# AdaLN block with attention on one core: first weights in chunks, TensorE multiplies zeros until they come, new order of work up to the first scores

## The reference

```python
mod = (silu(c) @ wmod).reshape(4, 6, 1, 512)          # sa, ca, ga, sb, cb, gb
h = layernorm(x) * (1 + ca) + sa
q = rope(h @ Wq.T);  c_kv = h @ Wdk.T                 # Wdk: 512 x 512
k = rope parts from h @ Wkr.T, the rest from c_kv @ Wupk.T
v = c_kv @ Wupv.T
x = x + ga * (softmax(causal(q @ k.T) / sqrt(128)) @ v) @ Wo.T
h = layernorm(x) * (1 + cb) + sb
x = x + gb * (h * sum(top8 of softmax(router)) + chosen weights @ expert_bias)
```

## Time and profile before

| | us |
|---|---|
| median of three runs | 1457.12 |
| the runs | 1459.28, 1457.12, 1456.52 |
| span of the profiled execution | 1457.5 |
| TensorE busy | 1430.5 (98%) |
| VectorE, ScalarE, GpSimd busy | 1153.7, 1006.8, 1023.1 |
| chain that ended last, TensorE's share | 85% |

### The profile page before, as it was taken

One profiled execution on the slowest core, in us unless ns is written; L12 is line 12 of the kernel. 1 busy time (PEld: TensorE's weight loads), 2 busy tenths in 40 slices (PEclk: granted clock), 3 DMA queues, 4 the chain that ended last, 5 costly groups with the idle time before them and its releaser, 6 DMA issues.

```text
span 1457.5 us, 24651 instructions
## 1 busy us (share of the span) xinstructions
PE 1430.5 (98%) x7150; PEld 1208.2 (83%) x7150; DVE 1153.7 (79%) x3544; ACT 1006.8 (69%) x2389; POOL 1023.1 (70%) x805
## 2 busy tenths in 40 slices
PE   7989999999999999999999999999999999999998
PEld 7877888888888888888888888888888888888886
DVE  5697777777777777787777777777779998998876
ACT  5667666776776676767676677677677676776674
POOL 3767766876776677667676767677588888887662
PEclk9999999999999999999999999999999999999999
DMA  9478765875677667676677667758788899889872
GB/s 305 157 210 250 225 193 182 239 235 152 204 227 218 187 212 228 190 206 211 184 216 233 220 180 208 202 178 257 228 239 259 269 295 262 284 256 270 270 229 67
DMA packets 215157, 322.03 MB, mean 221 GB/s; under 512 B 42512, under 2 KB 132464, under 8 KB 215024
## 3 DMA queue, kind: packets, MB, share of 16 engines
q1 hardware_dynamic: 214736, 320.39, 73.7%
q10 hardware_dynamic: 288, 0.07, 0.0%
HBM read 179.43 MB, written 140.95 MB: 220 GB/s over the span
## 4 chain that ended last, share of the span: by engine, by line
PE 85%; POOL 4%; DVE 4%; DMA 2%; issue 2%; ACT 2%; SPq 0%; DVEq 0%; ACTq 0%
PE bank_s L634 22%; PE bank_o L794 21%; PE bank_pv L744 14%; PE bank_s L700 13%; PE bank_s L666 5%; PE bank_s L651 5%; POOL PT_lo L1836 2%; PE bank_s L696 1%; PE bank_s L607 1%; PE bank_s L850 1%; DVE y L1540 1%; DMA PT_raw<-blocks 1%; POOL qT_lo L1829 1%; DMA wc_scratch<-wc_out 1%; DVE blocks L1488 0%
## 5 line engine op out<-in xcount | busy, mean ns | idle before, releaser
L1836 POOL TENSOR_TENSOR PT_lo<-PT_raw,PT_hi 128x640 fp32r<-128x640 f32 x246 | 382.2, 1576 | 30.4 <-ACT PT_hi L1126 30.4
L1112 ACT ACTIVATE probs<-probs,row_inv 128x512 f32<-128x512 f32 (+3 forms) x512 | 257.8, 553 | 192.1 <-DVE row_inv L1471 192.1
L1824 POOL TENSOR_TENSOR rot_c<-rot_c,rot_s 128x512 f32<-128x512 f32 x128 | 167.7, 1310 | 257.7 <-DVE rot_s L1428 257.7
L1105 ACT ACTIVATE probs<-probs,row_min 128x384 f32<-128x384 f32 (+3 forms) x512 | 281.6, 552 | 49.2 <-DVE row_min L1464 49.2
L1488 DVE STREAM_TRANSPOSE blocks<-probs 128x384 f32<-128x384 f32 x508 | 213.7, 446 | 21.2 <-ACT probs L1112 13.0
L700 PE MATMUL bank_s<-kT_both,qT_hi 128*128 128x512 f32 (+2 forms) x768 | 215.2, 341 | 3.0 <-issue 1.3
L1464 DVE CUSTOM_DVE_ANT_0 probs<-bank_s,mask 128x512 f32<-128x512 f32 (+2 forms) x384 | 205.5, 552 | 0.8 <-issue 0.3
L1829 POOL TENSOR_TENSOR qT_lo<-rot_c,qT_hi 128x512 fp32r<-128x512 f32 x128 | 167.0, 1304 | 51.0 <-ACT qT_hi L1087 50.2
L634 PE MATMUL bank_s<-hT_lo,wq_hi 128*128 128x512 f32 x484 | 194.8, 403 | 2.2 <-DVE row_min L1464 1.4
L794 PE MATMUL bank_o<-wo_lo,OT_hi 128*128 128x512 f32 x496 | 195.1, 393 | 0.5 <-DVE rot_s L1428 0.5
L794 PE MATMUL bank_o<-wo_hi,OT_hi 128*128 128x512 f32 x496 | 193.4, 390 | 0.0
(11 more groups left out here) (315 smaller groups left out, 3255.0 us busy)
## 6 DMA issues: line engine op xcount, KB each, us to landing
blocks<-blocks SPq DMA_DIRECT2D x127, 640.0 KB, 3.5
PT_raw<-blocks SPq DMA_DIRECT2D x500, 160.0 KB, 3.9
stage<-in_wq SPq DMA_DIRECT2D x32, 256.0 KB, 5.1
vblocks<-kv_raw SPq DMA_DIRECT2D x32, 256.0 KB, 5.4
kv_raw<-vblocks SPq DMA_DIRECT2D x128, 64.0 KB, 2.3
stage<-in_wo SPq DMA_DIRECT2D x32, 256.0 KB, 5.1
split_wq<-wq_hi SPq DMA_DIRECT2D x32, 256.0 KB, 5.4
split_wq<-wq_lo SPq DMA_DIRECT2D x32, 256.0 KB, 5.7
```

The lines of the kernel that those rows point to most:

```text
L1105: ins = act.activation(row(t, qt), row(t, qt), ACT.Exp, bias=row_min[m][:, qt:qt + 1], scale=-1.0, accum_out=row_sum[m][:, qt:qt + 1])
L1112: ins = act.activation(row(t, qt), row(t, qt), ACT.Copy, scale=row_inv[t % 2][:, qt:qt + 1])
L1824: pool.tensor_tensor(rot_c[:], rot_c[:], rot_s[:], ALU.add).then_inc(pool_a, 1)
L1836: pool.tensor_tensor(lo[:, at], raw_of(t)[:, at], hi[:, at].bitcast(F32), ALU.subtract).then_inc(pool_t, 1)
```

## The change

It touches only the stretch before the loop.

1. The first quarter of Wup is loaded in four chunks (SyncE), Wdk in four chunks of 128 columns instead of 128 rows, the first of them on ScalarE's queue. The splits follow chunk by chunk: up 0, down 0, up 1, 2, 3, down 1, 2, 3. `combine(0)` starts with the first two.
2. VectorE clears `kv_rot` first, and TensorE multiplies its zeros 9 times (fp32, 128 x 128) before `combine(0)`.
3. The exponential for silu and what follows it stand behind the splits. `ident` is loaded by SyncE, later.
4. All lists are rewritten up to `scores(2)`; `transpose_h(4)` to (7), `statistics(1)` to (3), `normalise_x(1)` to (3) and the loads of x stand later, combines and the first keys and queries earlier. Beyond `combine(15)` the lists are as they were.

```diff
+WARM_UPS = 9
+UP_FIRST, DOWN = [1, 3, 4, 5], [2, 6, 7, 8]
...
 def h_bank(n):
-    return bank["s1" if n % 2 == 0 else "o2"] if n < 2 * CH else bank["o2" if n % 2 == 0 else "o3"]
+    if n < 2 * CH:
+        return bank["o2" if n % 2 else "s1" if n < CH else "o3"]
+    return bank["o2" if n % 2 == 0 else "o3"]
...
+def warm_up():
+    pe.wait_ge(dve_pro, 1)
+    for _ in range(WARM_UPS):
+        pe.matmul(bank["pv"][:, 0:P], kv_rot[:, 0:P], kv_rot[:, P:2 * P], start=True, stop=True)
 def combine(i):
-    if c == 0:
-        pe.wait_ge(split_lo, n + 1 + (CH if n > 0 else 0))
+    if n == 0 and c > 0:
+        pe.wait_ge(split_lo, DOWN[c])
+    elif c == 0 and n > 0:
+        pe.wait_ge(split_lo, 2 * CH + n)
     for m in range(CH):
         if i == 0:
-            pe.wait_ge(split_lo, m + 2)
+            pe.wait_ge(split_lo, max(UP_FIRST[m], DOWN[0]))
...
+def split_down(c):
+    cols = slice(c * P, (c + 1) * P)
+    act.wait_ge(d_wdk[c], 16)
+    act.activation(wdk[0][:, :, cols], wdk_in[:, :, cols], ACT.Copy).then_inc(split_w, 1)
```

More of the change, by code:

```diff
@@ L586, in transpose_h @@
                     pe.wait_ge(d_ident, 16)
+                if n == CH:
+                    pe.wait_ge(dve_kr, 1)
                 if n == 2 * CH:
@@ L919, in tensor_program @@
             combine(2)
+            combine(3)
+            combine(4)
             modulation(0)
-            combine(3)
+            combine(5)
+            combine(6)
             modulation(1)
@@ L1253, in scalar_program @@
             combine(1)
-            normalise_x(0)
             combine(2)
             combine(3)
+            combine(4)
+            normalise_x(0)
+            combine(5)
+            combine(6)
+            split_first(0)
+            split_up(2)
             split_h(0)
[L1258 to L1261, removed]
             split_h(1)
[L1263 to L1266, removed]
             combine(7)
             split_first(1)
+            split_h(2)
+            split_h(3)
             combine(8)
+            combine(9)
             split_first(2)
[L1271 to L1274, removed]
             split_up(3)
-            split_h(6)
             k_split(0)
+            normalise_x(1)
+            combine(10)
+            q_split(0)
             split_first(3)
             split_first(4)
-            combine(10)
-            q_split(0)
-            split_h(7)
+            q_split(1)
+            split_h(4)
+            split_h(5)
             combine(11)
-            q_split(1)
-            split_first(5)
             exponentials(0, 0)
             exponentials(0, 1)
+            split_first(5)
             combine(12)
+            split_h(6)
+            split_h(7)
             normalise(0, 0)
             normalise(0, 1)
-            normalise_x(3)
+            normalise_x(2)
             q_split(2)
@@ L1299, in scalar_program @@
             q_split(3)
+            normalise_x(3)
             split_h(8)
@@ L1696, in vector_program @@
             modulate_h(0)
+            modulate_h(1)
+            split_up(2)
+            modulate_h(2)
+            modulate_h(3)
             statistics(1)
[L1698 to L1704, removed]
             dve.wait_ge(dve_pro, ROT_CLEAR)
@@ L1707, in vector_program @@
             k_rope(0)
-            modulate_h(6)
             dve.wait_ge(d_const, 64)
             q_rope(0)
-            modulate_h(7)
-            statistics(3)
+            split_up(3)
             q_rope(1)
-            split_up(3)
+            modulate_h(4)
+            modulate_h(5)
             mask_and_max(0, 0)
             mask_and_max(0, 1)
+            statistics(2)
             q_rope(2)
@@ L1719, in vector_program @@
             invert_sums(0, 1)
+            modulate_h(6)
+            modulate_h(7)
             transpose_blocks(0)
@@ L1722, in vector_program @@
             mask_and_max(1, 1)
+            statistics(3)
             q_rope(3)
```

150 lines of the change are left out of this document (83 added, 67 removed).

## The result

| | before | changed |
|---|---|---|
| median, us | 1457.97 (6 runs, 1456.52 to 1459.51) | 1462.28 (6 runs, 1460.67 to 1464.89) |
| span of the profiled execution | 1457.5 | 1459.6 |
| TensorE busy | 1430.5 | 1433.2 |

The ratio is 1.0028, interval 1.0017 to 1.0038: slower by 4.3 us in the medians, where 2.1 us less were forecast.

The account below looks back on a forecast made before the run. TensorE was taken as the bound: its moment past 117.22 plus a fixed 1340 us. A 5.5 us lead, less 0.9 and 0.9, plus 0.8, less 2.4, left 2.1: 1457.1 - 2.1 = 1455.0 us, range 1451.2 to 1458.4.

Parts of the forecast that it names:

- The 2.6 us for the zeros: Before combine(0): nine zero products raise TensorE's clock early, saving 2.6 us of slow matmuls, within bounds of 0 to 2.8.
- q_rope(1) runs from 46.3, mask_and_max(0) 49.9 to 51.8: New lists before scores(2): start of q_rope(1) and VectorE's next step, in us, after normalise_x(1) delays q_split(0) on ScalarE.
- plus 0.8 of short waits around 54 to 59 that are no longer there: Term of the sum: TensorE's short waits at 54 to 59 us vanish, adding 0.8 us to the lead.
- Plus a fixed rest of 1340 us: After TensorE's wait at 117.22: the remaining time was taken as a constant 1340 us, whatever the start gains.
- a pause of 1 us: TensorE's pause between zeros and combine(0): no row showed such a pause in the loop bringing slow matmuls back.
- Only the loads decide: Rival, chance 0.12: the wait at 117.22 hangs on load_transposed(0), only 0.7 us ahead, giving 1456.4 us.
- Slower: Rival, chance 0.09: narrow packets and a later list place make x 0 late, delaying combine(15); 1460.6 us.

Follow-up runs that it names:

- e4: The changed kernel with GpSimd's low part of the fifth weight piece moved ahead of q_rope(1); 1460.81 us, ratio 1.0008.
- e5: The changed kernel run again unaltered, in a later comparison against the kernel before; 1463.18 us, ratio 1.0035.
- e11: The kernel before with only GpSimd's fifth weight piece moved behind q_rope(1), as in the changed list; 1464.28 us, ratio 1.0041.
- e10: The kernel before with 64 waits on a finished load added at SyncE's step 20, nothing changed ahead of 117; 1458.21 us, ratio 1.0000.
- f3: The changed kernel with constant products filling TensorE's pauses at k_proj(0), q_proj(2) and near 92, 96 and 117 us; 1460.56 us, ratio 1.0011.
- e1: The kernel before with only the early clearing of kv_rot and the nine zero products added; 1459.98 us, ratio 1.0006.
- f1: The kernel before with constant products filling TensorE's three pauses near 93, 97 and 117 us; 1458.83 us, ratio 0.9999.
- e7: The changed kernel with SyncE's load_transposed(0) moved ahead of the store of combine(15); 1461.73 us, ratio 1.0025.
- f2: The changed kernel's start (chunks, slices, zeros) with the old lists, TensorE's pauses near 91, 95 and 116 us filled; 1459.65 us, ratio 1.0006.
- f4: The changed kernel with GpSimd's fifth piece ahead of q_rope(1), pauses at k_proj(0) and near 91, 95, 116 us filled; 1460.95 us, ratio 1.0015.
- e6: The changed kernel with ScalarE's normalise_x(3) moved behind combine(15); 1462.89 us, ratio 1.0030.

## Why the prediction was wrong

**The start: right, in part by luck.** combine(0) 5.91 (6.9), zeros ended before it, one table load, combine(2) ended at 12.8 (13.1), transpose_h(0) 23.51 (23.9), x in time, combine(8) and k_proj(0) waited 0.63 and 1.67 and ran at 28.43 and 34.54 (29.1, 34.2). The 2.6 us for the zeros was too much: 1.1. combine(0) started 1.0 us earlier than forecast, but combine(1) had to wait until 8.50 for the low part of its slice; these two errors largely cancel at 12.8. And about 1 us of the gain was the baseline's: the profile from which it was counted reached combine(3) at 19.84, others of that start at 18.75 to 19.15.

**The lists: the first failed step.** It is "q_rope(1) runs from 46.3, mask_and_max(0) 49.9 to 51.8", and the sum's "plus 0.8 of short waits around 54 to 59 that are no longer there". The step followed VectorE and ScalarE and left GpSimd's next entry out: the fifth piece stands behind q_rope(1) in the new list, and q_proj(2) waits for it. The short wait of 0.38 there did not vanish, it became 2.57. Alone, that order is worth 0.8 to 1 us at 117 (e4 against the changed kernel and e5, whose starts agree within 0.2 us), and in the kernel before it cost 5.6 us (e11). The other part is q_rope(1) itself, 48.09, of which GpSimd's sum of 2.81 us beside VectorE's split explains some 1.0 of 1.8. That contention stands in every trace, the one before included (54.26); no edit tried it. Instead of 2.1 us, 0.1 to 0.3 were left at 117 against the first profile, and none against e10.

**"Plus a fixed rest of 1340 us": the second failed step, and the larger error** (the forecast missed by 6.4 us, 2.0 of them at 117). The sum counted a wait at its own length and took the rest as the same for every start. It is not. A pause of TensorE like that of 2.57 us can bring the lower clock level for 3.4 us, 1.7 us of work lost, and in the first profiles the changed kernel has three pauses above 1.7 us (2.57, 1.76, 1.86) where the one before has one (1.75). With all pauses filled 1.8 us of the 4.3 and 5.4 were left (f3), the changed kernel's own median 1.7 and 2.6 lower. The forecast looked for slow products behind a pause of 1 us, saw none, and did not ask again for 2.5 us. What is left beside the clock, 1.8 to 2.8 us, has no shown cause. Some units of the loop wait for GpSimd's keys in one execution and not in another, 0.9 and 1.2 us at 898 and 1250 between the first two profiles; but e5 has no wait at 1250, and profiles with the old lists have late keys too (e10, e11, e1, f1). 0.3 us lie outside the span, where the changed kernel takes 1.65 us and the one before 1.32.

**The rivals.** "Only the loads decide" was near in one point: load_transposed(0) left at 77.32, no earlier than before. But e7 shows that an issue 1.8 us earlier moves the landing and the wait at 117 by only 0.1 us. "Slower" was given for a late x 0; it was never late, and the slower result came by a way that no rival named.

No version beat the kernel before. f1, which fills its pauses, is level (0.9999).

## What to carry over

When lists are reordered, follow each new list entry to who waits for it, on the idle engines too, and give every new pause of TensorE a second price: the clock behind it. Where the pause can't go, products of a constant into a bank that is about to be overwritten can keep the clock: in f3 they did in all 11 executions and delayed nothing at 117, in f2 and f4 they did not pay. A tuned loop with half a microsecond of slack on one engine is not a constant, and one profile is one execution: two of the same work differed here by 1 us at 117 and by 1.6 us at the end, as much as the gain that was forecast. Take a second profile of the kernel before ahead of counting such a gain.

## What the runs showed of the hardware

- The lower level (granted 0.50, products 0.43 us apart against 0.23) came in pieces of 3.4 us behind, or beginning in, pauses of 1.84 us and more (11 of 28 above 1.7 us, none of 40 from 1.2 to 1.7), in some executions and not in others of the same kernel: the changed kernel's wait of 2.57 us at 53 brought it in e6 and not in the first profile.
- A two-input instruction of 1.3 us that GpSimd started under VectorE's two-input split of Wup (1.76 us alone) ended 1.13 to 1.16 us after the split in all 18 traces, and so took up to 2.84 us. Where GpSimd's instruction was running first, the split was the longer one (2.29 us at 42.51).
- With an instruction fetch among them, eight issues on SyncE took 5.19 us against 3.63, in the median of 18 traces 4.6 against 3.6. The Trainium skill (Runtime: NRT & Kernel Launch, Instruction fetch mechanics) has the cost of a fetch mostly hidden; these rows don't agree, and they decide.
